# Twenty-eight row-wise units of 64 with some of their sums on VectorE, and a dense layer cut into seven pieces

## What is computed

```python
e = jnp.stack([tbl_0[ids[:, 0]], ..., tbl_31[ids[:, 31]]], axis=1)      # 1024 x 32 x 64
p, q = e[:, ROW_IDX], e[:, COL_IDX]                                      # 1024 x 496 x 64
z = jnp.einsum('bne,hne,bnh->bn', p, kernel, q)                          # 1024 x 496
h = jnp.concatenate([z, dense_ctx], axis=1)                              # 1024 x 512
h = jnp.maximum(h @ W_top1 + b_top1, 0.0)                                # 512 wide
h = jnp.maximum(h @ W_top2 + b_top2, 0.0)                                # 256 wide
y = h @ W_top3
```

## Time and profile before

| | us |
|---|---|
| median of three runs | 456.35 |
| the profiled execution | 456.08 |
| its span, first to last instruction | 454.3 |
| TensorE (PE) matmuls busy | 405.6 (89%) |
| VectorE (DVE) busy | 328.3 (72%) |
| ScalarE (ACT) busy | 266.0 (59%) |
| mean granted TensorE clock | 0.996 |

### The profile page before, as it was taken

One profiled execution on the slowest core, in us unless ns is written; L12 is line 12 of the kernel. 1 busy time (PEld: TensorE's weight loads), 2 busy tenths in 40 slices (PEclk: granted clock), 3 DMA queues, 4 the chain that ended last, 5 costly groups with the idle time before them and its releaser, 6 DMA issues.

```text
span 454.3 us, 9504 instructions
## 1 busy us (share of the span) xinstructions
PE 405.6 (89%) x3168; PEld 235.5 (52%) x3168; DVE 328.3 (72%) x354; ACT 266.0 (59%) x2085; POOL 242.5 (53%) x260
## 2 busy tenths in 40 slices
PE   0225799999989999999989999999989999999986
PEld 0113355555555666655455666655555656655555
DVE  1124499989888665899888665899888665899830
ACT  1000496559844754659845754659845754659841
POOL 5777777777777777777777777777300000000000
PEclk9999899999999999999999999999999999999999
DMA  5777891111111111111111111111000000000000
GB/s 123 159 172 160 198 239 28 28 28 26 28 29 30 28 28 28 26 28 27 28 27 29 28 27 29 29 27 28 17 1 3 2 2 0 1 1 2 2 1 0
DMA packets 13634, 19.28 MB, mean 42 GB/s; under 512 B 5585, under 2 KB 6929, under 8 KB 13585
## 3 DMA queue, kind: packets, MB, share of 16 engines
q1 hardware_dynamic: 5392, 10.27, 9.6%
q0 software_dynamic: 8192, 8.40, 9.4%
HBM read 18.65 MB, written 0.00 MB: 41 GB/s over the span
## 4 chain that ended last, share of the span: by engine, by line
PE 77%; DVE 8%; POOL 6%; issue 5%; DMA 2%; ACT 1%; DVEq 0%
PE bil L489 34%; PE z_ps L509 19%; PE bil L474 12%; POOL gathered L325 6%; PE side_ps L533 5%; DVE prod L418 4%; PE side_ps L538 2%; PE bil L533 2%; DMA gathered<-in_tbl,ids_sb 1%; DVE rows_prod L409 1%; PE bil L457 1%; DVE prod L425 1%; PE bil L538 1%; PE z_ps L523 1%; DVE inner L429 1%
## 5 line engine op out<-in xcount | busy, mean ns | idle before, releaser
L343 ACT ACTIVATE rows_prod<-rows_prod 128x64 f32<-128x64 f32 x1024 | 245.3, 243 | 127.3 <-DVE rows_prod L409 126.6
L325 POOL DMA_INDIRECT gathered<-in_tbl,ids_sb x256 | 242.3, 946 | 80.4 <-issue 77.8
L418 DVE TENSOR_TENSOR prod<-bil,emb 128x1024 f32<-128x1024 f32 x160 | 191.6, 1219 | 46.3 <-PE bil L489 46.3
L489 PE MATMUL bil<-emb,k_sb 64*128 64x256 f32 x1536 | 199.8, 393 | 7.3 <-DVE emb L397 5.1
L343 ACT ACTIVATION_READ_ACCUMULATOR rows_prod<-rows_prod 128x1 f32 x1024 | 193.6, 189 | 0.0
L489 PEld LDWEIGHTS bil<-emb,k_sb 64*128 64x128 f32 x1536 | 144.6, 191 | 87.0 <-issue 43.9
L509 PE MATMUL z_ps<-prod,sel_sb 128*32 128x512 f32 x704 | 102.5, 606 | 0.6 <-DVE prod L418 0.6
L409 DVE TENSOR_TENSOR rows_prod<-bil,gathered 128x1024 f32<-128x1024 f32 x64 | 77.8, 1216 | 18.4 <-PE bil L474 18.4
L474 PE MATMUL bil<-k_sb,emb 64*128 64x512 f32 x256 | 68.9, 616 | 0.9 <-DVE prod L418 0.9
L457 PE MATMUL bil<-ident_sb,gathered 64*128 64x64 f32 x256 | 14.7, 237 | 35.1 <-DMA gathered<-in_tbl,ids_sb 35.1
L397 DVE COPY emb<-bil 128x512 f32<-128x512 f32 x32 | 21.8, 680 | 31.3 <-PE bil L457 31.3
(11 more groups left out here) (25 smaller groups left out, 68.5 us busy)
## 6 DMA issues: line engine op xcount, KB each, us to landing
k_sb<-in_k_blocks SPq DMA_DIRECT2D x24, 256.0 KB, 5.0
gathered<-in_tbl,ids_sb POOLq DMA_INDIRECT x256, 2.5
k_sb<-in_k_blocks SPq DMA_DIRECT2D x8, 192.0 KB, 5.9
inner<-in_dense_rows SPq DMA_DIRECT2D x64, 1.0 KB
w_sb<-in_w SPq DMA_DIRECT2D x1, 1024.0 KB
k_sb<-in_k_blocks SPq DMA_DIRECT2D x8, 64.0 KB, 4.8
w_sb<-in_w SPq DMA_DIRECT2D x1, 512.0 KB
ids_sb<-in_ids SPq DMA_DIRECT2D x1, 128.0 KB, 2.1
```

The source lines that it names most:

```text
L325: pool.indirect_dma_start(gathered[:, q % 2, t, field * EMBED:(field + 1) * EMBED], None, tables[field], bass.IndirectOffsetOnAxis(ap=ids_ ...
L343: last = act.activation(row, row, ACT.Copy, accum_out=z_rows[:, t, half, col + x:col + x + 1])
L418: dve.tensor_tensor(out, x_y[:, :, :], both.to_broadcast([P, 2, BANK]), ALU.mult)\
L489: last = pe.matmul(out[:, s, i * CHUNK:(i + 1) * CHUNK], k_sb[rows, n, :], e[rows, j, :], start=True, stop=True)
```

## The change

`BATCH_PAIRS` now gives 28 batch units in a chunk, so 36 others and 18 reductions. The new batch units are 5, 7, 10, 11, 13, 14, 17, 19, 21, 23, 26, 27, 29, 31, 32, 34, 37, 39, 41, 43, 45, 47, 50, 52, 54, 57, 59 and 61. Bank 0 of `z_ps` is complete with the reduction of unit 59, the next reduction stands in unit 63, the chunk's last and `turn` in unit 2 of the next chunk as before.

After units 10, 15, 20, 25, 30, 35 and 40 VectorE sums the latest batch unit (10, 14, 19, 23, 29, 34 and 39) with `tensor_reduce`; ScalarE keeps the other 21. The 16 columns of a unit are no longer always adjacent, so 3 of a chunk's 7 VectorE sums are two instructions. At the same units TensorE does one of seven pieces of the previous chunk's dense layers (four of layer 1, two of layer 2, layer 3). The ring of rows has 4 slots, that of `prod` 6.

In the last chunk half of layer 1 (the groups of `z_sb` from bank 0) is issued ahead of the last reduction and `turn`, the relus are split between ScalarE and VectorE, and layer 2 begins with the first of them.

```diff
-BATCH_PAIRS = [0, 0, 1, 1, 1, 1, 2, 2]
+BATCH_PAIRS = [0, 0, 1, 2, 2, 3, 3, 3]
...
-BIL_RING, PROD_RING, ROWS_RING, IN_RING = 3, 7, 3, 4
+SUM_UNITS = [10, 15, 20, 25, 30, 35, 40]
+VECTOR_SUMS = {max(v for v in range(NB) if BATCHED[v] <= u) for u in SUM_UNITS}
+NV, NA = len(VECTOR_SUMS), NB - len(VECTOR_SUMS)
+BIL_RING, PROD_RING, ROWS_RING, IN_RING = 3, 6, 4, 4
...
-PIECES = ["l1a", "l1b", "l2", "l3"]
-KEPT_BEFORE = [0, 2, 4, 6]
+PIECES = [(1, n) for n in range(MT1)] + [(2, n) for n in range(MT2)] + [(3, 0)]
...
+PIECE_UNITS = [10, 15, 20, 25, 30, 35, 40]
+HEAD_AT = {(q + 1) * NU + u: (q, i) for q in range(CHUNKS - 1) for i, u in enumerate(PIECE_UNITS)}
...
             def sum_rows(u):
                 q, (_, part, t) = u // NU, UNITS[u % NU]
                 v = batched_before(u)
+                if v % NB in VECTOR_SUMS:
+                    return
...
+            def free_rows(v):
+                if v % NB in VECTOR_SUMS:
+                    dve.wait_ge(vector_summed, vector_sums_before(v) + 1)
+                else:
+                    dve.wait_ge(rows_summed, v - vector_sums_before(v) + 1)
+            def sum_rows(v):
...
+                dve.wait_ge(unit_multiplied, u + 1)
+                if q:
+                    dve.wait_ge(turned, q)
+                first = 0
+                while first < 16:
+                    half, col = batch_place(part, first)
+                    count = min(16 - first, LEFT - (col - (32 - LEFT)) % 32)
+                    last = dve.tensor_reduce(z_rows[:, t, half, col:col + count],
+                                             rows_prod[:, v % ROWS_RING, first:first + count, :], AXIS.X, ALU.add)
+                    first += count
+                last.then_inc(vector_summed, 1)
...
                 multiply(u)
+                if u % NU in SUM_UNITS:
+                    sum_rows(u // NU * NB + max(v for v in range(NB) if BATCHED[v] <= u % NU))
...
-                pe.wait_ge(rows_summed, (q + 1) * NB)
+                pe.wait_ge(rows_summed, (q + 1) * NA)
+                pe.wait_ge(vector_summed, (q + 1) * NV)
...
+            pe.wait_ge(z_copied, 2 * q + 1)
+            pe.wait_ge(head_kept, q * KEPT)
+            for n in range(MT1):
+                if n:
+                    pe.wait_ge(unit_multiplied, NUNIT - 2 + (n - 1) // 2)
+                for g in range(2):
+                    first_layer(n, g)
             for b in range(BATCHES * CHUNKS):
                 if reduce_unit(b) >= NUNIT:
                     reduce_batch(b)
+            pe.wait_ge(z_copied, 2 * q + 2)
+            for n in range(MT1):
+                first_layer(n, 2)
+                first_layer(n, 3).then_inc(head_done, 1)
             pe.wait_ge(unit_multiplied, NUNIT)
+            for g in range(MT1):
...
+                for n in range(MT2):
+                    second = pe.matmul(last_banks[MT1 + n][:, 0:CHUNK], w2_sb[:, g, n * P:(n + 1) * P], h1_sb[:, g, :],
+                                       start=g == 0, stop=g == MT1 - 1)
```

More of the change, by code:

```diff
@@ L93, in batched_before, with vector_sums_before @@
     return q * NB + sum(1 for v in BATCHED if v < r)
+def vector_sums_before(v):
+    q, r = divmod(v, NB)
+    return q * NV + sum(1 for x in VECTOR_SUMS if x < r)
 def unit_at(a):
@@ L130, in slot_row, with batch_place @@
     return slot // 64, 32 * (s % 4) + 2 * (s // 4)
-def batch_place(first):
-    at = FIRST_PARTS.index(first)
-    return at // 4, 32 * (at % 4) + 32 - LEFT
+def batch_place(first, x):
+    half, r = divmod(16 * FIRST_PARTS.index(first) + x, 4 * LEFT)
+    return half, 32 * (r // LEFT) + 32 - LEFT + r % LEFT
 def z_row(b, side):
@@ L144, in z_row @@
         if first in FIRST_PARTS:
-            half, row = batch_place(first)
-            return 2 + half, row + 8 * s + 4 * (part - first) + 2 * i + side
+            half, row = batch_place(first, 8 * s + 4 * (part - first) + 2 * i + side)
+            return 2 + half, row
     u = [v for v in range(NU) if UNITS[v][:2] in (("inner", part), ("fields", part))][0]
@@ L190 @@
 REDUCED_AT = {reduce_unit(b): b for b in range(BATCHES * CHUNKS) if reduce_unit(b) < NUNIT}
-PIECES = ["l1a", "l1b", "l2", "l3"]
-KEPT_BEFORE = [0, 2, 4, 6]
+PIECES = [(1, n) for n in range(MT1)] + [(2, n) for n in range(MT2)] + [(3, 0)]
 KEPT = 7
-HEAD_AT = {reduce_unit((q + 1) * BATCHES + 2 * i + 3): (q, i) for q in range(CHUNKS - 1) for i in range(len(PIECES))}
+LAST_KEPT = 4
+PIECE_UNITS = [10, 15, 20, 25, 30, 35, 40]
+HEAD_AT = {(q + 1) * NU + u: (q, i) for q in range(CHUNKS - 1) for i, u in enumerate(PIECE_UNITS)}
 USES = []
@@ L260, in interaction_tower @@
         head_kept = sem("head_kept")
+        vector_kept = sem("vector_kept")
         y_stored = sem("y_stored")
+        last_pairs = [bil[BANKS_OF["unit", u]] for u in range(NUNIT - 3, NUNIT)]
+        last_banks = [side_ps[:, :]] + [pair[:, x, :] for pair in last_pairs for x in range(2)]
         block = ctx.enter_context(nc.Block())
@@ L339, in sum_rows @@
                     act.wait_ge(turned, q)
-                half, col = batch_place(part)
                 for x in range(16):
                     row = rows_prod[:, v % ROWS_RING, x, :]
-                    last = act.activation(row, row, ACT.Copy, accum_out=z_rows[:, t, half, col + x:col + x + 1])
+                    half, col = batch_place(part, x)
+                    last = act.activation(row, row, ACT.Copy, accum_out=z_rows[:, t, half, col:col + 1])
                 last.then_inc(rows_summed, 1)
@@ L357, in keep_head @@
                 act.wait_ge(head_done, q * len(PIECES) + i + 1)
[L358 to L366, removed]
+                layer, n = PIECES[i]
+                if layer == 1:
+                    act.activation(h1_sb[:, n, :], bank, ACT.Relu, bias=b1_sb[:, n:n + 1]).then_inc(head_kept, 1)
+                elif layer == 2:
+                    act.activation(h2_sb[:, n, :], bank, ACT.Relu, bias=b2_sb[:, n:n + 1]).then_inc(head_kept, 1)
                 else:
@@ L384, in _ @@
             copy_z(CHUNKS - 1, 1)
-            for i in range(len(PIECES)):
-                keep_head(CHUNKS - 1, i, bil[i % BIL_RING][:, 0, :])
+            done = (CHUNKS - 1) * len(PIECES)
+            for n in (0, 2):
+                act.wait_ge(head_done, done + n + 1)
+                act.activation(h1_sb[:, n, :], last_banks[n][:, 0:CHUNK], ACT.Relu, bias=b1_sb[:, n:n + 1])\
+                   .then_inc(head_kept, 1)
+            act.wait_ge(head_done, done + MT1 + 1)
+            act.activation(h2_sb[:, 0, :], last_banks[MT1][:, 0:CHUNK], ACT.Relu, bias=b2_sb[:, 0:1]).then_inc(head_kept, 1)
+            act.wait_ge(head_done, done + MT1 + MT2 + 1)
+            act.activation(y_sb[:, (CHUNKS - 1) * CT:TILES], last_banks[MT1 + MT2][:, 0:CT], ACT.Copy).then_inc(head_kept, 1)
         @block.vector
@@ L437, in _ @@
                 multiply(u)
+                if u % NU in SUM_UNITS:
+                    sum_rows(u // NU * NB + max(v for v in range(NB) if BATCHED[v] <= u % NU))
+            done = (CHUNKS - 1) * len(PIECES)
+            for n in (1, 3):
+                dve.wait_ge(head_done, done + n + 1)
+                dve.tensor_scalar(h1_sb[:, n, :], last_banks[n][:, 0:CHUNK], b1_sb[:, n:n + 1], 0.0, ALU.add, ALU.max)\
+                   .then_inc(vector_kept, 1)
+            dve.wait_ge(head_done, done + MT1 + 2)
+            dve.tensor_scalar(h2_sb[:, 1, :], last_banks[MT1 + 1][:, 0:CHUNK], b2_sb[:, 1:2], 0.0, ALU.add, ALU.max)\
+               .then_inc(vector_kept, 1)
         @block.tensor
@@ L527, in head @@
             def head(q, i, bank):
-                if PIECES[i] in ("l1a", "l1b"):
+                layer, n = PIECES[i]
+                if layer == 1:
                     pe.wait_ge(z_copied, 2 * q + 2)
[L530 to L539, removed]
+                    for g in range(GROUPS):
+                        last = pe.matmul(bank, w1_sb[:, g, n * P:(n + 1) * P], z_sb[:, g, :],
+                                         start=g == 0, stop=g == GROUPS - 1)
+                elif layer == 2:
+                    for g in range(MT1):
+                        last = pe.matmul(bank, w2_sb[:, g, n * P:(n + 1) * P], h1_sb[:, g, :],
+                                         start=g == 0, stop=g == MT1 - 1)
                 else:
@@ L564, in _, with first_layer @@
                     side_head(u)
-            last = CHUNKS - 1
+            q = CHUNKS - 1
+            def first_layer(n, g):
+                return pe.matmul(last_banks[n][:, 0:CHUNK], w1_sb[:, g, n * P:(n + 1) * P], z_sb[:, g, :],
+                                 start=g == 0, stop=g == GROUPS - 1)
+            pe.wait_ge(z_copied, 2 * q + 1)
[5 more added lines that the diff above has]
+                    first_layer(n, g)
             for b in range(BATCHES * CHUNKS):
@@ L568, in _ @@
                     reduce_batch(b)
+            pe.wait_ge(z_copied, 2 * q + 2)
+            for n in range(MT1):
+                first_layer(n, 2)
```

(21 more changed lines are left out.)

17 lines of the change are left out of this document (11 added, 6 removed).

## The result

The changed kernel takes 477.44 us, the median of four runs (476.68 to 479.02), against 456.17 us: a ratio of 1.047, 95% interval 1.045 to 1.049. The forecast was 473.9 with a range of 465 to 480. The profiled execution of the changed kernel is the slowest of its four, 479.02 us, with a span of 477.2.

A forecast was written before the change was run, and what follows sets the result against it. TensorE was taken as the bound before the change, with ScalarE's late sums deciding `turn` after it. By differences 454.3 + 4.8 + 18.9 - 11.1 + 9.9 - 4.9 = 471.9; the forecast was 471.8 + 1.78 + 0.27 = 473.9 us, range 465 to 480.

The forecast's parts named there:

- The start, up to A of chunk 0: From the start to the end of VectorE's half of chunk 0's unit 41: VectorE-bound, 106.4 against 101.6, +4.8.
- A to B: From the end of VectorE's unit 41 to `turn`: ScalarE's ten sums make it 40.9 against 34.6, +6.3, three times.
- The low clock: Behind TensorE's 7-us wait in unit 63: half speed for 4.2 us, +2.0.
- two grounds for this term: For the low clock: granted 0.50 behind 4.16 us idle in chunk 0; a fields unit at 28.96 taking 2.08.
- B to A: From `turn` to the end of VectorE's next unit 41: four reductions fewer, 63.5 against 67.2, -3.7, three times.
- lost to a thin lead: Between `turn` and VectorE's next unit 41: TensorE's lead of two units is thin against sums of 1.2, +0.4.
- The last chunk: From the end of VectorE's last unit 41 to the last `turn`: ScalarE's last sum decides, 39.4 against 29.5, +9.9.
- the end: Behind the last `turn`: layer 1 is 3.6 shorter and gaps between layers shrink, 12.8 against 17.7, -4.9.
- The rival with the clock up: At the waits in unit 63: TensorE keeps its clock, 3 x 1.5 less, 469.4 us; chance 0.22.
- the one in which VectorE takes over: VectorE's sums cost 2.4 each, so it bounds chunk 0 and `turn` to the next unit 41: 499 us; chance 0.05.
- The rival in which ScalarE isn't late: From VectorE's unit 41 to `turn`: the ten sums overlap more, TensorE bounds it at 32.2, 435.5 us; chance 0.05.

The follow-up runs named there:

- early copy: Changed kernel with ScalarE's copy of bank 0 of `z_ps` ahead of the sum of unit 54, not behind that of unit 57: 477.61 us against 477.4.
- half sums: Changed kernel with ScalarE summing only 8 of the 16 rows of each of its units from 41 on: 444.69 us.
- filler: Changed kernel with seven matmuls of 512 columns on constants ahead of TensorE's wait for the copy in unit 63, results unused: 471.51 us.
- pieces away: Changed kernel with the seven dense pieces at units 12, 17, 22, 27, 32, 37 and 39, away from VectorE's sums: 485.78 us.

## Why the forecast was right, and where its sizes were off

*The start, up to A of chunk 0* (+4.8 forecast, +6.5 measured). VectorE is the bound, as forecast, with a price a little under mine (1.13 apart, 1.18 where in two pieces, for 1.2). What the term left out is the slow clock. Four of the kernels above are the same program up to A of chunk 0 (early copy, half sums, filler, pieces away), so there are five executions to read. From unit 10's product to A three of them take 47.8 us at full clock; the forecast had 48.2. The changed kernel's profile and that of the pieces away take 49.3, at a mean clock of 0.965:

```profile
91.00:95.00 4.00, 3.41 (x16) 1.38 (x16) 3.49 (x4) 4.00 (x36) 3.08 (x4) 0.57 0.17 37
93.60 1.65 PE L570 MATMUL z_ps<-prod,sel_sb 128*32 128x512 f32 x8
95.18 1.13 PE L535 MATMUL bil<-k_sb,emb 64*128 64x512 f32 x4
96.36 1.22 DVE L436 TENSOR_TENSOR rows_prod<-bil,gathered 128x1024 f32<-128x1024 f32 x1 [1.42 <-ACT rows_prod L366]
```

The last row, VectorE's product of unit 34, names ScalarE as what it waited for, but it isn't the ring of rows. The slot was unit 27's; ScalarE summed unit 27 from 88.6 to 92.4. It is TensorE's half of unit 34, done at 96.31, behind a unit and a reduction at the slow clock. In the other execution with this loss the same wait is put down to TensorE:

```profile
95.00 1.23 DVE L436 TENSOR_TENSOR rows_prod<-bil,gathered 128x1024 f32<-128x1024 f32 x1 [1.39 <-PE bil L535]
```

At full clock (early copy, half sums, filler) it is 0.43. The rest of the term is the execution's own: unit 10's product starts between 55.9 and 59.1 us in the five (58.81 in the changed kernel's, 58.24 in the forecast's row), and A lies between 103.7 and 108.1. The forecast's 106.4 is inside that, and the profile that was compared is the latest of the five.

*A to B* (+6.3 forecast, +7.4 measured). Ten sums, the copy, the 6-us wait and the loss of clock are as forecast: TensorE idle for 6.16 us where I had 7. ScalarE's own queue ends a little sooner than I had it: with the clock kept (filler) or lost elsewhere (early copy) B is at A + 38.87, not 39.4. The low clock was mis-sized. From the reduction in unit 63 to B it is 7.55 us with the filler (forecast 7.5) and 10.6 in the changed kernel (forecast 9.5): the clock costs 3.0 where I had 2.0, because it comes twice, behind the wait and again from 146 to 149.4, and I had one stretch of 4.2 us. The early copy prices it the same, at 2.9. Of the forecast's two grounds for this term one doesn't hold: for the unit of 2.08 us at 28.96 the trace before gives a granted clock of 1.00 from 28.9 to 31, so that row doesn't show a loss of clock.

*B to A* (-3.7 forecast, -3.5 measured). TensorE's four reductions fewer are there: 15 to 11, 67.35 to 63.9. From 67.35 the forecast's sum without a lost lead gives 63.25, and the kernel without VectorE sums has 63.3. What I called lost to a thin lead, 0.4, is 0.5. The term owes its size to the place of the pieces: 2.3 more without it.

*The last chunk* (+9.9 forecast, +9.4 measured) is ScalarE's queue, and the end (-4.9 both) went as forecast:

```profile
464.41 1.08 PE L585 MATMUL z_ps<-ident_sb,z_rows 128*32 128x128 f32 x32 [0.33 <-ACT rows_prod L366]
466.21 1.13 PE L628 MATMUL side_ps<-z_sb,w_sb 128*128 128x256 f32 x4 [0.72 <-ACT z_sb L376]
469.77 3.62 PE L652 MATMUL bil<-h_sb,w_sb 128*128 128x256 f32 x16
474.06 1.02 PE L660 MATMUL bil<-w_sb,h_sb 128*128 128x1 f32 x8 [0.67 <-DVE h_sb L497]
```

Layer 2 begins 3.56 us behind layer 1's second half, with no gap; 8.08 before.

In sum, from the forecast's 471.8 to 477.2: 1.7 at the start, 3 x 1.0 between A and B, 3 x 0.4 between B and A, -0.5 in the last chunk. These sizes are of the slowest of the four runs, 479.0; the median is 477.4 against the forecast's 473.9. The rival with the clock up (469.4) is refuted by every run of the changed kernel (mean clock 0.950 to 0.957, against 0.996 before), and the one in which VectorE takes over by its sum at 1.2 us, not 2.4. The rival in which ScalarE isn't late gave 435.5; taking half of its late sums away gave 444.7, so the gain that it stood for was there.

## What to carry to other kernels

Where work moves to an engine with room on the average, lay its new queue out between the two points at which others wait for it, and count there: ScalarE at 71% of the span was the bound, by ten sums of 3.83 us in a stretch of 34.5, and three sums moved out of that stretch by one list were worth 27 us. A small instruction that others wait for, here a copy of 0.6 us, inherits the whole queue ahead of it; moving it alone moves the wait. And idle time of TensorE cost more here than itself, so that a filler of constants in the gap can pay.

## What the runs showed of the hardware

- Filling a gap of 6 us with matmuls whose results nobody reads took 5.9 us off the kernel. The granted clock is at 0.50 within such a gap (137 to 139) and still for 3.1 us after work resumes; one such wait, with the loss of clock paid in full, cost 2.9 us more than its idle time (early copy).
- The clock was also lost without a long idle time: 0.57 in 91 to 95, where TensorE had just waited for VectorE in gaps of 0.58 and 1.13 us. Of five executions of the same program up to there, two lost it and three kept 1.00; the filler's has gaps of 0.57 and 1.13 at this place and kept it. The Trainium skill (TensorE: Matmul & The Clock Gate, the section on psum-queue depth-cycling) names such losses from frequent small idle times, in another kernel and in bf16. The trace agrees that they occur; it doesn't show what decides between one execution and the next.
- The spread of a kernel's runs follows the mean clock. With the filler, 6.3 us lie between the runs at 0.996 and 0.982. As the low level is half the full one, (1 - mean clock) of the span is an upper bound for what a run lost, by my estimate; between these two runs it differs by 6.6 us.
